# Macaron block: the loads of k and q in the attention stage are begun by ScalarE instead of SyncE

## What is computed

```python
x = x + 0.5 * ffn(layernorm(x), weight, bias, centroids, assignments)
x = x + attn(layernorm(x), Wq, bq, Wk, bk, Wv, bv)
x = x + 0.5 * ffn(layernorm(x), ...)          # the same weights again

# ffn: a dense layer 1024 -> 1024, masked by rows and by columns
dots = softmax(x @ centroids.T / 0.1)         # 64 clusters
query_sel = any(dots > 0.01, over clusters); cluster_sel = any(dots > 0.01, over all tokens)
out = where(query_sel[:, None] & cluster_sel[assignments][None, :], x @ weight.T + bias, 0)

# attn: D = 32, HEADS = 32, 8 heads of k and v; softmax over the 32 x 32 products of D, per token and head
q = einsum('bse,edh->bsdh', x, Wq) + bq       # k and v the same way, repeated 4 times
scores = einsum('bsdh,bseh->bsde', q, k) / sqrt(D)
out = einsum('bsde,bseh->bsdh', softmax(scores), v)
```

## Time and profile before

| | |
|---|---|
| profiled execution | 1196.15 us, its span 1194.3 us |
| median of 3 runs | 1196.13 us |
| TensorE (PE) busy | 1181.7 us, 99% |
| VectorE (DVE) busy | 799.3 us, 67% |
| ScalarE (ACT) busy | 499.2 us, 42% |
| GpSimd (POOL) busy | 441.0 us, 37% |
| DMA, all queues | 208.73 MB, mean 175 GB/s |

### The profile page before, as it was taken

How to read it: one execution, slowest core, us unless ns; L and a number is a source line. 1 busy time by engine, 2 the same in 40 slices (tenths; PEclk the granted TensorE clock), 3 DMA queues, 4 the chain that set the end, 5 groups by cost and what they waited for, 6 DMA issues and landing times.

```text
span 1194.3 us, 24986 instructions
## 1 busy us (share of the span) xinstructions
PE 1181.7 (99%) x10072; PEld 1002.5 (84%) x10072; DVE 799.3 (67%) x1272; ACT 499.2 (42%) x718; POOL 441.0 (37%) x582
## 2 busy tenths in 40 slices
PE   7999999999999999999999999999999999999998
PEld 6888888888888888888888888888888878888887
DVE  6654554455444477787777877778777774199987
ACT  5232233222211355656656656565565663211110
POOL 1335445543424643433434334344343210051332
PEclk9999999999999999999999999999999999999999
DMA  8578777876565366565565666565655565017885
GB/s 275 144 206 232 207 206 193 225 211 182 164 189 159 98 169 169 148 171 146 160 166 139 181 152 152 160 155 164 161 142 164 129 169 193 2 72 259 279 304 195
DMA packets 344978, 208.73 MB, mean 175 GB/s; under 512 B 289440, under 2 KB 308640, under 8 KB 344864
## 3 DMA queue, kind: packets, MB, share of 16 engines
q1 hardware_dynamic: 329696, 187.73, 56.2%
q10 hardware_dynamic: 15168, 19.40, 4.7%
HBM read 118.49 MB, written 88.60 MB: 173 GB/s over the span
## 4 chain that ended last, share of the span: by engine, by line
PE 91%; DMA 3%; DVE 2%; issue 1%; ACT 1%; SPq 1%; POOL 1%; POOLq 0%; DVEq 0%
PE ps_b L285 9%; PE ps_q L285 8%; PE ps_q L287 8%; PE ps_q L286 8%; PE ps_b L287 8%; PE ps_b L286 8%; PE ps_a L285 8%; PE ps_a L287 8%; PE ps_a L286 8%; PE ps_t L292 6%; PE ps_q L1450 3%; PE ps_q L299 2%; PE ps_q L301 2%; PE ps_q L1425 2%; DMA y_scratch<-xa 1%
## 5 line engine op out<-in xcount | busy, mean ns | idle before, releaser
L318 POOL TENSOR_TENSOR var_eps<-moments,eps 128x1 f32<-128x1 f32 x96 | 18.2, 190 | 396.6 <-DVE moments L314 396.6
L285 PE MATMUL ps_a<-w_hi,odd_hi 128*128 128x512 f32 x368 | 147.7, 401 | 0.0
L287 PE MATMUL ps_a<-w_hi,odd_lo 128*128 128x512 f32 x368 | 143.8, 391 | 0.0
L286 PE MATMUL ps_a<-w_lo,odd_hi 128*128 128x512 f32 x368 | 143.2, 389 | 0.0
L635 POOL TENSOR_SCALAR f_out<-f_out,token_on 128x1024 f32<-128x1024 f32 x30 | 85.6, 2852 | 75.6 <-DVE f_out L1013 75.3
L686 POOL TENSOR_TENSOR x_ring<-x_ring,f_tmp 128x1024 f32<-128x1024 f32 x32 | 77.3, 2414 | 91.2 <-DVE best L1159 58.5
L285 PE MATMUL ps_b<-proj_hi,y_hi 128*128 128x512 f32 x256 | 103.3, 403 | 0.0
L287 PE MATMUL ps_b<-proj_hi,y_lo 128*128 128x512 f32 x256 | 100.0, 391 | 0.0
L286 PE MATMUL ps_b<-proj_lo,y_hi 128*128 128x512 f32 x256 | 99.7, 390 | 0.0
L327 ACT ACTIVATE y_tok<-x_ring,norms 128x1024 f32<-128x1024 f32 x64 | 79.7, 1245 | 38.0 <-ACT o_head L881 21.0
L737 POOL TENSOR_TENSOR late<-late,mask 128x1024 f32<-128x1024 f32 x18 | 44.1, 2463 | 137.3 <-DMA late<-x_scratch 91.6
(11 more groups left out here) (219 smaller groups left out, 3113.1 us busy)
## 6 DMA issues: line engine op xcount, KB each, us to landing
xa<-in_L_attn_x SPq DMA_DIRECT2D x32, 512.0 KB, 5.0
f_tmp<-f_scratch SPq DMA_DIRECT2D x32, 512.0 KB, 4.2
x_ring<-in_L_attn_x SPq DMA_DIRECT2D x32, 512.0 KB, 3.6
f_scratch<-f_out SPq DMA_DIRECT2D x30, 512.0 KB, 4.0
x_scratch<-x_ring SPq DMA_DIRECT2D x30, 512.0 KB, 3.5
y_scratch<-xa SPq DMA_DIRECT2D x28, 512.0 KB, 4.6
ya_tok<-y_scratch SPq DMA_DIRECT2D x112, 128.0 KB, 3.3
late<-x_scratch SPq DMA_DIRECT2D x22, 512.0 KB, 6.7
```

Of the source, the lines that this page charges most:

```text
L285: pe.matmul(acc, hi[:, k, :], w_h[:, k, cols], start=(k == 0), stop=False)
L286: pe.matmul(acc, hi[:, k, :], w_l[:, k, cols], start=False, stop=False)
L287: last = pe.matmul(acc, lo[:, k, :], w_h[:, k, cols], start=False, stop=(k == KB - 1))
```

## The change

In the attention loop SyncE no longer issues the loads of k and q. A new function `load_heads` on ScalarE holds the two waits and the two loads, and is called in step i for tile i-1, after the normalisation of the next tile (L937) and before `norm_again` and `copy_pair`. The pattern's name moves to where both engines see it.

```diff
@@ sync @@
                         sp.wait_ge(qk_read, t + 1)
                         sp.dma_start(qkv_d[t, 0:2 * HKV].rearrange("s k e -> k s e"),
                                      qkv_tok[:, 0:2 * HD].rearrange("p (s e) -> p s e", e=D)).then_inc(qk_stored, 16)
-                        sp.wait_ge(qk_stored, 16 * (t + 1))
-                        wait(sp, k_ready, t)
-                        sp.dma_start(k_head[:, :],
-                                     qkv_d[t, HKV:2 * HKV].rearrange(BY_TOKEN_GROUP, c=T4, j=2)).then_inc(k_in, 16)
-                        wait(sp, scores, t)
-                        sp.dma_start(q_head[:, :],
-                                     qkv_d[t, 0:HKV].rearrange(BY_TOKEN_GROUP, c=T4, j=2)).then_inc(q_in, 16)
                         if 1 <= i < 5:
                             store_tail(i)
                         sp.wait_ge(v_read, t + 1)
@@ scalar @@
+                def load_heads(t):
+                    act.wait_ge(qk_stored, 16 * (t + 1))
+                    wait(act, k_ready, t)
+                    act.dma_start(k_head[:, :],
+                                  qkv_d[t, HKV:2 * HKV].rearrange(BY_TOKEN_GROUP, c=T4, j=2)).then_inc(k_in, 16)
+                    wait(act, scores, t)
+                    act.dma_start(q_head[:, :],
+                                  qkv_d[t, 0:HKV].rearrange(BY_TOKEN_GROUP, c=T4, j=2)).then_inc(q_in, 16)
+
...
                         normed(act, y_tok[:, :], x_ring[i % RING][:, :], 1, i).then_inc(y2, 1)
+                    if 0 <= i - 1 < NT:
+                        load_heads(i - 1)
                     if NT <= i < NT + 2:
                         norm_again(i - NT)
```

More of the change, by code:

```diff
@@ L329, in macaron_kernel @@
         BY_TILE = "p (t c) -> p t c"
+        BY_TOKEN_GROUP = "g (c x j) e -> x g c (j e)"
         PAIR = [P, 2, NCL]
@@ L518, in load_x @@
                         sp.dma_start(x_ring[t % RING][:, :], x2_d[2 * (t - NT) + 1]).then_inc(again_in[t - NT], 16)
-                BY_TOKEN_GROUP = "g (c x j) e -> x g c (j e)"
                 for i in range(0, NT + 3):
```

## The result

The changed kernel takes 1215.2 us (median of 4 runs, 1214.65 to 1215.73), the kernel before beside it 1196.24: a ratio of 1.0155, 95% interval 1.0137 to 1.0172, 1.6% slower. The forecast was 1211, range 1202 to 1217. One execution of a later experiment (thirteen copies) ran at a mean granted clock of 0.85 instead of 1.00 and took 1306.0 us; its ratio leaves it out.

The account below looks back on a forecast made before the run. TensorE, busy 99% of the span, was taken as the bound. Stalls of 9.4 us in even steps, 2.2 in odd steps and 3.4 in step 32 gave 15.0 us on 1196.15: forecast 1211 us, range 1202 to 1217.

Parts of the forecast that it names:

- TensorE bounds the loop, and the change can only lose: Whole loop: TensorE is busy 99% of the span, so SyncE's shorter wait gains 0; slower was given 0.88.
- ScalarE is held, y_hi is 0.61 us late, and VectorE passes it on: End of ScalarE's step 14: wait and two issues delay y_hi 0.61 us, passed through VectorE to TensorE's cluster logits.
- 0.15 us of slack at L299, stalls of 0.46 us a pair, 9.4 us over the even steps, with four long ones: Cluster logits after 13 even steps, 6 to 30: lateness less slack stalls TensorE; steps 6, 16, 20, 30 lose more.
- Odd steps 2.2 us: Issues ahead of ScalarE's pair-sum copy delay the fold: 1.16 us in step 15, less in 5, 11, 25; between 0 and 5.
- Step 32, 3.4 us: The new wait and issues precede the normalisation into f_tmp, which TensorE's transposes need: one stall of 3.4 us.
- What is removed costs and brings nothing: SyncE loses a 2.7 us wait and two issues a step; later DMAs move forward about 1.2 us; gain 0.
- Queues in each other's way: Rival: ScalarE's q issue waits about 0.6 us every step for SyncE's store of v; 1222 us, chance 0.06.
- the lock on the shared block: Rule weighed: sequencers share the descriptor generator under a lock, so ScalarE's issues could wait for SyncE's; the trace spoke against it.

Follow-up runs that it names:

- thirteen copies: Kernel before, all DMAs on SyncE; ScalarE ends its step waiting for the q and k store, then making thirteen one-column copies: 1207.0 us, ratio 1.0102.
- only q on ScalarE: Changed kernel, but SyncE keeps the k load; ScalarE issues only q, in steps 32 and 33 after f_tmp is filled: 1195.3 us, ratio 1.0006.
- f behind q: Changed kernel, with SyncE's load of the next f held until q has landed: 1212.0 us, ratio 1.0147; in a second set 1213.9, ratio 1.0159.
- side-by-side pair: Changed kernel and the same with f's load waiting for q, on one chip: 1216.7 us, ratio 1.0184, against 1213.9 us, ratio 1.0159.
- f_tmp first: Changed kernel, but in steps 32 and 33 ScalarE fills f_tmp before waiting for the store and loading k and q: 1216.0 us, ratio 1.0170.
- f ahead of k: Kernel with ScalarE issuing only q, and SyncE issuing the store of v and load of next f ahead of k: 1233.0 us, ratio 1.0320.

## Why the prediction was right, and where it was not

- *TensorE bounds the loop, and the change can only lose.* Right: no experiment came out faster, and only q on ScalarE changed nothing.
- *ScalarE is held, y_hi is 0.61 us late, and VectorE passes it on.* Right: 0.62 in step 14. The hold without a DMA shows that this is a cause by itself: 13.0 us. The pair of steps was to take 37.5 us instead of 37.0; with f behind q the usual pairs take 37.5, and in the changed kernel pairs take 37.5 to 39.2, 38.0 in the mean.
- *0.15 us of slack at L299, stalls of 0.46 us a pair, 9.4 us over the even steps, with four long ones.* Right where nothing else stands in front: with f behind q the waits at L299 are 10.3 and 10.5 us in two executions, 0.26 to 0.50 in the usual pairs, and the long ones are in steps 7, 11, 17, 21 and 31 (1.7, 1.4, 1.7, 1.0, 1.1 in the first). The second execution has long ones in steps 11, 17, 21, 27 and 31: five each time, not four. In the changed kernel the scores (7.7) and L299 (6.0) share them. I had read the long issues from single rows and was not sure that they recur; mostly they do, at the same steps.
- *Odd steps 2.2 us.* 0.9 and 1.7 in two executions, nearly all in step 15.
- *Step 32, 3.4 us.* 2.9 to 3.1 in all five traces that have it.
- *What is removed costs and brings nothing.* This is the step that failed. I moved SyncE's f forward by 1.2 us and looked only at who waits for f, not at what it runs beside. It met q: landing 5.0 instead of 2.7 us. By the side-by-side pair it costs about 2.8 us, not clear of noise, and 1.7 to 2.7 by the traces, some of it in steps 2 and 4, where VectorE had slack and L299 is not yet in the way (1.2 us each at the scores in the changed kernel's trace).
- *The clock was not in the sum.* The stretch at the lower level behind the stall of step 32 is worth some 1.7 us in the execution shown.

With these the sum closes. Set beside the trace of the kernel before, start by start, the loop of the profiled execution takes 19.8 us more: the scores 7.7, L299 6.0 and the product behind it 0.9, f_tmp 3.1, the fold 0.9, the reduced clock 1.7 and a hole in step 13 with what follows it 0.7, together 21.0, less 1.1 for the hole in step 33 that only the trace of before had. The stages outside the loop take 0.9 us less, mostly because the wait of 1.1 us at L299 in the first stage is not in this execution. That leaves the 19.0 us of span.

That the time fell inside the range is in part luck. The sum of 15.0 us left out the collision and the clock, had 1.3 us too much for the odd steps and 0.3 for step 32, and 1 us too little at L299; what it left out fitted into the 6 us between the forecast and the top of the range.

- *Queues in each other's way.* As I put it, an issue held up by the other queue's issue, it was wrong in the usual step: the issues grew by 0.03 to 0.05 us. But three of the four long issues of q have one of f beside them that is as long; in step 6 ScalarE's q takes 1.74 us from 489.80 and SyncE's f 1.75 from 489.91. In the kernel before, where SyncE alone issues all of them, the same steps had a long issue: q in steps 6, 16 and 30, and in step 26 the store of v, 1.48 us. With only q on ScalarE it was the store of v that took 1.5 to 1.8 us in steps 16, 26 and 30. So neither sharing nor the load of q is needed for a long issue; they come at certain places in the program, for a reason that stays open. The contention that mattered was one stage further, in the transfers. The rule of the Trainium skill that I had weighed, the lock on the shared block (page "Perfetto Trace Analysis", section "DMA Instruction — HWDGE (DVE, Sync)"), is neither shown nor excluded by this.

Open: what makes single issues take 1.4 to 1.8 us, and single landings of the store 3.3 to 4.5, mostly at the same steps in both kernels; and what the collision costs in time beyond the noise of the runs.

## What to carry to other kernels

Before moving a wait and its DMAs to another engine, find the hole in that engine's timeline and compare it with wait plus issues plus the gap behind them: here 0.7 us were free, one issue fitted and two did not. Then ask of everything that stood behind the wait in the old list what it will run beside once it is early; a large load that nobody waits for can still delay the small one that TensorE waits for. When a stall is taken away, look for the same lateness at the next station before counting the gain.

## What the runs showed of the hardware

- A DMA issue holds ScalarE's computation: in the changed kernel y_hi starts 0.03 to 0.05 us after the end of the q issue in every even step from 2 to 30, long issues of 1.4 to 1.8 us included.
- Nearly the same stall, 2.9 to 3.1 us at f_tmp in step 32, was followed by a stretch below full clock in three executions (granted clock 0.72 over 6 us in the changed kernel; 0.66 over the 5 us that hold it with f behind q the second time and with thirteen copies) and by full clock in two others (1.00 throughout in the changed kernel's second execution, and in the first with f behind q). Such a drop costs some 1.7 us in each of the three, and makes part of the scatter between runs of one kernel.
- Shorter stalls were followed by it too: 2.0 us at the scores in step 11 of the run with f_tmp first (granted clock 0.67 over the 5 us from 576), and 1.8, 2.0 and 2.1 us in the run with f ahead of k, while there stalls of 2.7 and 2.4 us were not. In these traces the length of the stall does not tell whether the clock falls.
- Thirteen ScalarE copies of one column each follow each other every 0.1 us, though each is shown as 0.19 us long.
